# Attention and ternary feed-forward layer on one core: weights loaded ahead of the angle tables, tables turned one chunk at a time, prefetches placed behind the first stacks, later geometry behind the row maxima

## What is computed

```python
q = rope(xn @ Wq)           # 8 heads of 32
k = rope(xn @ Wk)           # 2 key heads of 32, each shared by 4 query heads
v = xn @ Wv
out = softmax(causal(q @ k.T * 32**-0.5)) @ v
qp, kp = q[..., :3] @ dirs, k[..., :3] @ dirs       # one number per row and head
geo_out = softmax(causal(qp[:, None] * kp[None, :])) @ v
attention = (out + head_scales * (geo_out - out)) @ Wo
# ternary(W): W -> {-1, 0, +1} * mean(|W|); topk keeps the 102 largest of 1024 per row
hidden = topk(relu(xn @ ternary(W_syn).T + b_syn))
ffn = layernorm(xn + hidden @ ternary(W_out).T + b_out) * gamma + beta
```

## Time and profile before

| | |
|---|---|
| median of three runs | 775.68 us |
| the profiled execution | 776.62 us |
| its span, first to last instruction | 774.9 us |
| mean granted TensorE clock | 0.927 |
| PE busy | 694.9 us (90%) |
| DVE, ACT, POOL busy | 498.3, 449.4, 226.8 us |
| first matmul | at 18.8 us |
| first row-maximum matmul | at 64.3 us |
| DMA | 35.46 MB in 26931 packets |

### The profile page before, as it was taken

How to read it: one execution, slowest core, us unless ns; L and a number is a source line. 1 busy time by engine, 2 the same in 40 slices (tenths; PEclk the granted TensorE clock), 3 DMA queues, 4 the chain that set the end, 5 groups by cost and what they waited for, 6 DMA issues and landing times.

```text
span 774.9 us, 12300 instructions
## 1 busy us (share of the span) xinstructions
PE 694.9 (90%) x4424; PEld 327.5 (42%) x4424; DVE 498.3 (64%) x974; ACT 449.4 (58%) x733; POOL 226.8 (29%) x304
## 2 busy tenths in 40 slices
PE   0857988799999999969999999999999989998993
PEld 0533444334244443423343444554544445654532
DVE  3782786856675876558567696567665567767602
ACT  1655345344334442468444445799989989996550
POOL 3431314531111212111010120452343453247232
PEclk9965899679899998989999999999989999999996
DMA  9494038240000000160000000000000000000000
GB/s 238 150 280 134 1 128 209 77 102 1 1 7 1 1 1 1 32 158 1 0 3 3 1 1 3 22 22 28 28 22 22 28 22 28 16 22 8 1 1 27
DMA packets 26931, 35.46 MB, mean 46 GB/s; under 512 B 7090, under 2 KB 21298, under 8 KB 26483
## 3 DMA queue, kind: packets, MB, share of 16 engines
q1 hardware_dynamic: 21874, 33.80, 15.0%
...
...
## 4 chain that ended last, share of the span: by engine, by line
PE 62%; DVE 10%; issue 5%; ACT 3%; POOL 3%; DMA 3%; SPq 1%; DVEq 0%; ACTq 0%; POOLq 0%
PE acc L1420 14%; PE acc L1413 14%; PE side L1312 10%; PE scores L1395 7%; DVE piece_max L1126 4%; PE scores L1399 3%; DMA q_stack<-q_parked 3%; PE side L1366 2%; PE side L1357 2%; PE side L1374 2%; PE side L1367 2%; ACT probs L889 2%; PE side L1349 2%; PE side L1350 1%; POOL probs L746 1%
## 5 line engine op out<-in xcount | busy, mean ns | idle before, releaser
L889 ACT ACTIVATE probs<-scores 128x1024 f32<-128x1024 f32 (+3 forms) x320 | 271.0, 893 | 230.9 <-PE acc L1420 208.3
L1126 DVE TENSOR_REDUCE piece_max<-side 128x1 f32<-128x512 f32 x189 | 125.3, 685 | 78.9 <-PE side L1312 77.5
L1413 PE MATMUL acc<-probs,v_nat 128*32 128x512 f32 (+3 forms) x1280 | 158.1, 568 | 8.7 <-POOL probs L746 8.5
L1420 PE MATMUL acc<-probs,ones_all 128*32 128x512 f32 (+3 forms) x1280 | 156.8, 564 | 0.0
L1312 PE MATMUL side<-k_stack,q_stack 96*128 96x512 f32 (+3 forms) x309 | 122.5, 450 | 17.0 <-DMA q_stack<-q_parked 9.2
L746 POOL TENSOR_SCALAR_AFFINE_SELECT probs<-probs 128x256 f32<-128x256 f32 x128 | 60.8, 484 | 243.8 <-ACT probs L889 242.5
L1312 PEld LDWEIGHTS side<-k_stack,q_stack 96*128 96x128 f32 x309 | 55.5, 199 | 106.2 <-issue 52.4
L1395 PE MATMUL scores<-q_stack,k_stack 98*128 98x512 f32 (+3 forms) x320 | 92.5, 393 | 1.5 <-ACT probs L889 1.3
L1129 DVE CUSTOM_DVE_ANT_0 side<-side,tail_mask 128x256 f32<-128x256 f32 (+3 forms) x120 | 57.7, 488 | 33.3 <-PE side L1312 32.8
L1413 PEld LDWEIGHTS acc<-probs,v_nat 128*32 128x32 f32 x1280 | 37.2, 114 | 86.9 <-issue 64.8
L1152 DVE RECIPROCAL d_raw<-d_raw 128x512 f32<-128x512 f32 x16 | 53.6, 3347 | 23.2 <-ACT o_raw L902 23.2
...
## 6 DMA issues: line engine op xcount, KB each, us to landing
q_stack<-q_parked SPq DMA_DIRECT2D x12, 512.0 KB, 8.0
q_parked<-turned SPq DMA_DIRECT2D x8, 512.0 KB, 3.0
...
res<-in_L_attn_x_dram SPq DMA_DIRECT2D x4, 512.0 KB, 8.9
x_parked<-xn SPq DMA_DIRECT2D x4, 512.0 KB, 3.2
xT_parked<-xnT SPq DMA_DIRECT2D x4, 512.0 KB, 5.2
xb<-x_parked SPq DMA_DIRECT2D x16, 128.0 KB, 2.0
```

The source lines that it names most:

```text
L889: nc.scalar.activation(probs[:, slot % 2, pair, :, off:], scores[:, pair, :, off:], ACT.Exp, scale=ATT_SCALE if kind == 0 else 1.0).then_i ...
L1126: free(nc.vector.tensor_reduce(piece_max[:, h, p:p + 1], pt, AX.X, ALU.max), ("S",) + a)
L1413: nc.tensor.matmul(acc[D * h:D * h + D, 0, off:], v_nat[:, j, g], probs[:, slot_no[a] % 2, h // 2, h % 2, off:], start=(j == 0), stop=(j = ...
L1420: last = nc.tensor.matmul(acc[D * h:D * h + D, 1, off:], ones[:, 0:D], probs[:, slot_no[a] % 2, h // 2, h % 2, off:], start=(j == 0), stop ...
```

## The change

1. ACT's queue issues Wq, Wk and Wv first, and then cos and sin of chunk 0 alone. SP issues x of chunk 0 and the small table and then waits until the projection weights are in; x of chunk 1, `W_syn` and the rest follow.
2. `angles` is a buffer of its own for one chunk. Angles of chunks 1 to 3 are loaded by SP (`ang_in`, two DMAs each) when the table units of the chunk before are done. The pictures are spread in the third part of `turned` instead of `probs`, so `spread` on POOL waits until all parked parts of the chunk before have landed. `t_put` writes `trig` directly and waits for the `rope` of the chunk before. `t_park` and `trig_in` are gone, three DMAs of 768 KB out and three in; so is a memset of `turned`.
3. `w_sort` gets rank 0.2, behind chunk 0's `shift`. `w_cut` is split in `w_mean` and `w_cut`, with the same five instructions.
4. For the planner, `w_next`, `xz_in` and `xb_in` follow `stack_lo` of chunk 0.
5. For the planner, the later statistics follow maxima two chunks back (`m`), and `geo_lo` and `scan` of chunk c follow the maxima of chunk c - 1. Assumed arrival times are changed.

The matmuls, exponentials and reductions are the same in number and size.

```diff
+        if c:
+            add("ang", "sp", 2, ("ang_in", c), 1100, [("unit", "tT", c - 1, 2)])
...
+            rank = 0 if c == 0 else 2 * c - 0.5
+            slots_free = [("khi_park", c - 1), ("klo_park", c - 1)] if c else []
+            add("spread", "act" if c == 0 else "pool", rank, ("spread", c, s), (650, 650, 900)[s] if c == 0 else (700, 700, 900)[s],
+                [("ang_in", c)] + turned[-2:-1] + slots_free)
-            add("trig", "act", rank, ("t_put", c, s), 600, [("unit", "tT", c, s)] + [("t_park", c - 1)] * (c > 1), empties=("tT", c, s))
+            add("trig", "act", rank, ("t_put", c, s), 600, [("unit", "tT", c, s)] + [("rope", c - 1, k) for k in "ABK"] * (c > 0),
+                empties=("tT", c, s))
             turned.append(("unit", "tT", c, s))
-        if c:
-            add("t_park", "sp", 0, ("t_park", c), 550, [("t_put", c, s) for s in range(3)])
-    add("w_sort", "dve", 0, ("w_sort",), 2000, [("w",)])
+    add("w_sort", "dve", 0.2, ("w_sort",), 2000, [("w",)])
...
-            add("stat", "dve", STAT_RANK if c else 0, ("stat", t), 650, [("x", c)])
+            add("stat", "dve", STAT_RANK if c else 0, ("stat", t), 650, [("x", c)] + [("m", c - 2)] * (c > 1))
...
-        if c:
-            add("trig_in", "sp", 1, ("trig_in", c), 550, [("t_park", c)] + [("rope", c - 1, s) for s in "ABK"])
...
+        due = [("m", c - 1)] if c else []
-        add("geo", "dve", rank, ("geo_lo", c), 1220, [("geo_hi", c)] + old)
-        add("geo", "dve", rank, ("scan", c), 2800, [("geo_in", c)] + old)
+        add("geo", "dve", rank, ("geo_lo", c), 1220, [("geo_hi", c)] + old + due)
+        add("geo", "dve", rank, ("scan", c), 2800, [("geo_in", c)] + old + due)
...
-            add("w", "sp", 0, ("w_next",), 500, [("w_cut", 0)])
+            add("w", "sp", 0, ("w_next",), 500, [("w_cut", 0), ("stack_lo", 0)])
...
+        add("w", "dve", 2, ("w_mean", m), 560, [("unit", "wsum", m)] + [("m", 0)] * m, empties=("wsum", m))
+        add("w", "dve", W_RANK, ("w_cut", m), 3900, [("w_mean", m)] + [("w_put", 0, 3)] * m)
...
-        add("xz", "sp", 3, ("xz_in", t), 550, [("xnT_park", c)] + [("xs_lo", t - 2)] * (t > 1))
+        add("xz", "sp", 3, ("xz_in", t), 550, [("xnT_park", c), ("stack_lo", 0)] + [("xs_lo", t - 2)] * (t > 1))
...
-        add("xb", "sp", 3, ("xb_in", t), 550, [("xn_park", c)] + [("y", t - 2)] * (t > 1))
+        add("xb", "sp", 3, ("xb_in", t), 550, [("xn_park", c), ("stack_lo", 0)] + [("y", t - 2)] * (t > 1))
...
+        angles = sb("angles", [P, TPC, ANG])
+        spread = turned[:, :, 2].rearrange("p b (t m) -> p b t m", m=P)
-        angles = flat[:, 0:NT * ANG].rearrange("p (t a) -> p t a", a=ANG)
-        w_given = flat[:, NT * ANG:NT * ANG + KC * QKV].rearrange("p (k n) -> p k n", k=KC)
-        trig_next = flat[:, 3 * CHUNK:6 * CHUNK].rearrange("p (s t) -> p s t", s=3)
-        spread = flat[:, 6 * CHUNK:8 * CHUNK].rearrange("p (b t m) -> p b t m", b=2, m=P)
+        w_given = flat[:, 0:KC * QKV].rearrange("p (k n) -> p k n", k=KC)
...
+            sp.dma_start(small[:], small_table.broadcast_to([P, H * 3 + RANKS])).then_inc(dir_in, 16)
+            sp.wait_ge(w_in, N_W_IN)
             sp.dma_start(res[:, TPC:2 * TPC], x_rows[1]).then_inc(x_in[1], 16)
-            sp.dma_start(small[:], small_table.broadcast_to([P, H * 3 + RANKS])).then_inc(dir_in, 16)
...
+                if k == "ang_in":
+                    sp.wait_ge(side_full, unit_no[("tT", c - 1, 2)] + 1)
+                    rows = slice(CHUNK * c, CHUNK * c + CHUNK)
+                    sp.dma_start(angles[:, :, 0:HALF], cos_table[rows, 0:HALF].rearrange("(t p) d -> p t d", p=P)).then_inc(ang_in, 16)
+                    sp.dma_start(angles[:, :, HALF:], sin_table[rows].rearrange("(t p) d -> p t d", p=P)).then_inc(ang_in, 16)
...
-                    consumed(sp, ("wsum", 0))
+                    sp.wait_ge(ternary_ready, 1)
...
-                    pool.wait_ge(ang_in, 32)
+                    pool.wait_ge(ang_in, 32 * (c + 1))
+                    pool.wait_ge(hi_out, 32 * c)
+                    pool.wait_ge(lo_out, 32 * c)
...
-            act.dma_start(angles[:, :, 0:HALF], cos_table[:, 0:HALF].rearrange("(t p) d -> p t d", p=P)).then_inc(ang_in, 16)
-            act.dma_start(angles[:, :, HALF:], sin_table.rearrange("(t p) d -> p t d", p=P)).then_inc(ang_in, 16)
             for w, at in ((Wq, 0), (Wk, H * D), (Wv, QK)):
                 act.dma_start(w_given[:, :, at:at + w.shape[1]], w.rearrange("(k p) n -> p k n", p=P)).then_inc(w_in, 16)
+            act.dma_start(angles[:, :, 0:HALF], cos_table[0:CHUNK, 0:HALF].rearrange("(t p) d -> p t d", p=P)).then_inc(ang_in, 16)
+            act.dma_start(angles[:, :, HALF:], sin_table[0:CHUNK].rearrange("(t p) d -> p t d", p=P)).then_inc(ang_in, 16)
...
-                    if c > 1:
-                        act.wait_ge(trig_out, 16 * (c - 1))
-                    free(nc.scalar.copy(trig[:, s] if c == 0 else trig_next[:, s], pt), ("tT",) + a)
+                    if c >= 1:
+                        for q_ in ("qA", "qB", "qK"):
+                            consumed(act, (q_, c - 1))
+                    free(nc.scalar.copy(trig[:, s], pt), ("tT",) + a)
...
-                    if c == 0:
-                        for i in range(3):
-                            consumed(dve, ("tT", 0, i))
-                    else:
-                        dve.wait_ge(trig_in, 16 * c)
+                    for i in range(3):
+                        consumed(dve, ("tT", c, i))
+                    if c >= 1:
...
```

More of the change, by code:

```diff
@@ L50 @@
 W_RANK = 3
+W_UNIT = 1.5
 Z_ACT = 1
@@ L102, in build_plan @@
             unit("proj", 2 * c, ("q" + s, c), 1790, [("xnT", c, 0), ("xnT", c, 1)] + [("w_sort",)] * (c == 0))
-            add("rope", "dve", 0 if c == 0 else ROPE_RANK, ("rope", c, s), 1250, [("unit", "q" + s, c)] + ([("trig_in", c)] if c else [("t_put", 0, s) for s in range(3)]) + parked,
+            add("rope", "dve", 0 if c == 0 else ROPE_RANK, ("rope", c, s), 1250, [("unit", "q" + s, c)] + [("t_put", c, i) for i in range(3)] + parked,
                 empties=("q" + s, c))
@@ L195, in build_plan @@
             add("exp", "act", 0, ("exp", c, g, kind, j, pair), 170 + 855 * share, [("score", c, g, kind, j, pair)]
-                + ([("sum",) + slots[n - 2]] if n >= 2 else [("t_park", NCH - 1), ("w_sort",)]))
+                + ([("sum",) + slots[n - 2]] if n >= 2 else [("w_sort",)]))
             if j >= TPC * c:
@@ L214, in build_plan @@
         add("dma", "sp", 0, ("store", t), 500, [("o_add", t), ("y_out", t)])
-    done = {("x", 0): 5500.0, ("x", 1): 11000.0, ("x", 2): 13500.0, ("x", 3): 15500.0, ("tables",): 9000.0, ("dir_in",): 14000.0}
-    done.update({("w",): 9000, ("late",): 24000, ("w_in", 0): 19000, ("w_in", 1): 19000})
+    done = {("x", 0): 5200.0, ("x", 1): 13000.0, ("x", 2): 19000.0, ("x", 3): 21000.0, ("ang_in", 0): 9500.0, ("dir_in",): 14000.0}
+    done.update({("w",): 11000, ("late",): 26000, ("w_in", 0): 18000, ("w_in", 1): 19000})
     emptied_by = {}
@@ L555, in spread_angles @@
         def spread_angles(copy, c, s):
-            buf, tiles = spread[:, spread_no[(c, s)] % 2], slice(TPC * c, TPC * c + TPC)
+            buf = spread[:, spread_no[(c, s)] % 2]
             if s < 2:
@@ L1003, in _ @@
             nc.vector.memset(q_geo[:].bitcast(F32), 0.0).then_inc(geo_filled, 1)
-            mark(nc.vector.memset(other[KROWS:, 2], 0.0))
             mark(nc.vector.memset(run_end[:, 0:1], -3.0e38))
@@ L1158, in _ @@
                     free(nc.vector.tensor_tensor(res[:, t], pt[:, 0:C], res[:, t], ALU.add), ("o", t))
+                if k == "w_mean":
+                    m = a[0]
+                    pt = filled(dve, ("wsum", m))
+                    free(nc.vector.tensor_scalar(w_scale[:, m:m + 1], pt[:, 0:1], 1.0 / (N * C), None, ALU.mult), ("wsum", m))
+                    consumed(dve, ("wsum", m))
+                    link(nc.vector.tensor_scalar(w_cut[:, 0:1], w_scale[:, m:m + 1], 1e-8, 0.5, ALU.add, ALU.mult))
+                    link(nc.vector.tensor_scalar(w_cut[:, 1:2], w_cut[:, 0:1], -1.0, None, ALU.mult))
                 if k == "w_cut":
                     m = a[0]
-                    pt = filled(dve, ("wsum", m))
                     if m == 1:
```

46 lines of the change are left out of this document (15 added, 31 removed).

## The result

| | before | after |
|---|---|---|
| median of ten runs | 776.41 us (773.15 to 788.14) | 771.37 us (768.97 to 775.22) |
| ratio after / before | | 0.9944, 95% interval 0.9919 to 0.9969 |
| profiled execution, span | 776.62, 774.9 us | 771.47, 769.3 us |
| mean granted clock | 0.927 | 0.913 |
| PE busy | 694.9 us | 710.9 us |

The medians are of all runs; a ratio and its interval leave out runs more than 1.5% above the fastest of their kernel.

A forecast was written before the change was run, and what follows sets the result against it. PE was taken as the bound, so start gains reach the end nearly whole: 9.0 + 2.0 - 1.0 + 3.5 + 5 = 18.5 us off 776.62, less 0.9, gives 757.2 us; range 741 to 770.

The forecast's parts named there:

- Term 1: At the start, ACT's first copy comes 9.0 us earlier than 18.05 us, bounds 6 and 12.
- Term 2: From ACT's first copy to `xnT`, 2.0 us less than the 10.5 us of before, bounds 1 and 3.
- Term 3: From `xnT` to the first row maximum, 1.0 us more; bounds 3 us less to 5 us more.
- Terms 4 and 5: More of chunk 1's work before the first row maximum, 3.5 us; fewer PE waits later on, 5 us.
- Term 4: Before the first row maximum: chunk 1's projections in, chunks 2 and 3's tables out; net 3.5 us, bounds 0 and 5.
- Rival B: Clock follows where PE's waits for stacks go, 64.3 to 100 and 133.2 to 160 us: 741 us, chance 0.15.
- Edits at nothing: Table transfers, new waits of `spread` and `t_put`, `xb` and split `w_cut` counted as no cost; `xb` at worst 5 us.
- Rivals C and D: C: ACT-bound feed-forward eats the gain, 773 to 778 us, chance 0.06; D: chunks 2 and 3 late, 792 us, 0.07.
- the 94% that was set as a sign: From 490 to 755 us, a PE busy share below 94% would show the prediction wrong.
- The signs that were to show the prediction wrong: PE waiting over 5 us for chunk 2/3 `q_stack`, ACT's first copy waiting beyond 12 us, or PE share under 94%.

The follow-up runs named there:

- experiments 1 and 2: experiment 1, and the changed kernel with 19 useless copies on ACT ahead of its first copy: 782.46 us, ratio 1.0074.
- experiment 1: The kernel before, its order of work kept but for one swap, with only the new start (weights before angles, SP's wait, angles split): 766.74 us, ratio 0.9892.
- experiment 3: The changed kernel with chunk 1's projections held behind chunk 0's maxima for the planner, all else re-planned: 767.56 us, ratio 0.9894.
- experiment 5: The changed kernel without the holds on geometry and statistics: 777.03 us; without the geometry's alone: 784.6; without the statistics' alone: 770.73.
- experiment 4: Chunk 0 matmuls issued twice: row maxima in the changed kernel, 773.47 us; row maxima in experiment 1's kernel, 773.65; geometric scores in the changed kernel, 772.15.

## Why the prediction was wrong

**Term 1** (9.0 forecast, bounds 6 to 12): 10.8 us. The quarter of the sin table landed 4.3 us after its issue, sooner than the middle of the bounds allowed for. The chunk loads cost nothing that shows, as the sum had it.

**Term 2** (2.0): `xnT` came 8.3 us after the first copy in place of 10.5, so 2.2 us.

**Term 3** (1.0 more): from `xnT` to the first row maximum it was 51.35 - 15.53 = 35.8 us in place of 35.7, so nothing was lost, and the first row maximum came 12.9 us early where 10 were forecast. The longer way from the last issue that the sum feared is there (41.63 to 51.35, 9.7 us in place of 7.6), but the last issue itself ended 2.0 us sooner after `xnT`.

These three pass to the end in experiments 1 and 2. Had the sum stopped here, it would have given 766 us, where experiment 1 was measured at 766.7.

**Terms 4 and 5** (8.5 us together) are the steps that failed. Their mechanism came true: chunk 1's projections run before the first maxima, from 130 to 200 us PE's idle time fell from 7.4 to 1.0 us, and chunk 3's wait from 5.12 to 1.78. The idle time fell by 21.6 us, more than the whole sum. But the sum counted every microsecond of idle time as a microsecond of the span, "with the same work done", and held the loss to the half clock constant. It rose from 43.0 to 57.6 us. With chunk 1's work ahead of chunk 0's maxima PE waits less and has the half clock for longer, and experiment 3 shows both sides of the trade at once: 14 us more idle time, 15 us less loss. Term 4 had priced even its own matmuls at the full clock: chunk 1's three projections took 7.54 us where 5.5 were counted, with the clock at 0.50 from 40 to 45 us.

**Rival B** had the right quantity and the wrong sign. It argued that where waits go, the clock stays up, for up to 16 us of gain. From 130 to 200 us that holds: the loss fell from 13.1 to 7.0 us. Elsewhere it rose by more. Windows of 5 us of after:

```profile
55.00:60.00 5.00, 5.00 (x18) 1.57 (x16) 2.43 (x7) 3.75 (x6) 2.66 (x4) 0.50 0.51 159
60.00:65.00 5.00, 5.00 (x25) 1.64 (x24) 1.87 (x10) 3.19 (x7) 1.98 (x4) 0.50 0.77 237
65.00:70.00 5.00, 4.80 (x20) 2.21 (x19) 2.94 (x13) 1.09 (x3) 0.77 (x2) 0.50 1.04 219
70.00:75.00 5.00, 4.90 (x26) 2.10 (x29) 3.37 (x14) 0.00 (x0) 0.00 (x0) 0.50 0.32 70
75.00:80.00 5.00, 4.45 (x35) 1.76 (x27) 3.80 (x13) 4.33 (x6) 1.22 (x3) 0.84 0.00 0
80.00:85.00 5.00, 5.00 (x23) 1.39 (x26) 4.89 (x6) 0.00 (x0) 0.41 (x1) 0.50 0.00 0
```

From 55 to 75 us PE is busy for 19.7 of 20 us and has the half clock all through, 1.2 GHz; and it falls back to it at 80 us behind a window in which it was busy for 4.45 of 5 us. The Trainium skill (TensorE: Matmul & The Clock Gate, HAM oscillation) puts the return to half clock down to waits for DMA between bursts of matmuls. The trace does not bear that out here. Before the clock fell between 50 and 55 us, PE had waited 0.76 us for a DMA (`q_geo`, at 50.92 us); from 55 to 86 us its waits are four for DVE, 0.7 us in all, the longest 0.2, and the clock fell again among them. So the rule, on which B was weighed, could not foresee the loss.

**Edits at nothing**: right for the prefetches in this list; `spread` on POOL cost PE 4.5 us of waiting, inside an idle time that still fell by what was forecast; wrong for the geometry's hold, which is worth 6 to 13 us (experiment 5). Two edits of the planner are in neither the list of the change nor the sum: the units `wsum` and `wT` went from rank 0 to 1.5, and `w_mean` of `W_out` waits for chunk 0's maxima. No run takes them back alone.

**Rivals C and D** did not come: experiment 1's gain arrived whole, and the longest wait for `q_stack` is 1.8 us. PE was busy for 250.50 us from 490 to 755, 94.5%, just above the 94% that was set as a sign:

```profile
490.00:755.00 265.00, 250.50 (x1789) 124.60 (x1787) 161.81 (x295) 210.85 (x380) 100.44 (x131) 0.97 0.06 19
```

The signs that were to show the prediction wrong thus all stayed away while it was wrong, since none of them looked at the clock.

**Open**: why the clock is lower with chunk 1's work ahead of the maxima. That it is, is shown from 65 to 130 us; after 350 us the cause is open. Thin work as the reason was tried and not settled (experiment 4).
